# A graph network on one core: 64-column products, kept sums in the messages' place, later layers written out on TensorE

## The reference, cut to what matters

```python
h = relu(layernorm(x))                      # x: 12500 x 64
for l in range(3):
    mlp = lambda z: relu(z @ W1[l] + b1[l]) @ W2[l] + b2[l]
    agg = segment_sum(mlp(h[dst]), src)     # 400000 edges
    h = mlp(h + agg)
out = x + h @ Wf + bf
```

## Time and profile before

| | us |
|---|---|
| median of 3 runs (2140.95 to 2144.04) | 2142.98 |
| the profiled execution | 2147.51 |
| its span | 2145.8 |
| around the span | 1.7 |

### The profile page before, as it was taken

One profiled execution on the slowest core, in us unless ns is written; L12 is line 12 of the kernel. 1 busy time (PEld: TensorE's weight loads), 2 busy tenths in 40 slices (PEclk: granted clock), 3 DMA queues, 4 the chain that ended last, 5 costly groups with the idle time before them and its releaser, 6 DMA issues.

```text
span 2145.8 us, 42350 instructions
## 1 busy us (share of the span) xinstructions
PE 1985.3 (93%) x16959; PEld 1076.8 (50%) x16959; DVE 1442.2 (67%) x1655; ACT 842.3 (39%) x2198; POOL 591.3 (28%) x270
## 2 busy tenths in 40 slices
PE   4566889999999999989999999999999999999998
PEld 3454445555555555544455455455445555555554
DVE  7999999999999999946643443343465444444343
ACT  5986888888888888812200000000010000000000
POOL 2666666666666766600000000000000000000000
PEclk9886999999999999999999999999999999999999
DMA  7356666666666666653544553543544555555452
GB/s 204 95 138 177 187 188 193 191 192 196 191 193 191 196 190 187 197 167 91 157 146 120 165 150 106 178 143 112 165 149 128 167 167 157 160 150 167 137 165 71
DMA packets 332835, 344.60 MB, mean 161 GB/s; under 512 B 21562, under 2 KB 303992, under 8 KB 332184
## 3 DMA queue, kind: packets, MB, share of 16 engines
q1 hardware_dynamic: 327516, 335.59, 54.0%
q0 software_dynamic: 2352, 6.43, 1.1%
q10 hardware_dynamic: 2816, 0.53, 0.2%
HBM read 252.58 MB, written 89.89 MB: 160 GB/s over the span
## 4 chain that ended last, share of the span: by engine, by line
PE 60%; DVE 23%; DMA 7%; issue 5%; POOL 2%; SPq 2%; ACT 1%; ACTq 1%; DVEq 0%; POOLq 0%
PE ps L1552 49%; DVE arena L756 13%; DMA arena<-counts_dram 7%; PE ps L1417 6%; DVE arena L764 5%; POOL arena L633 2%; DVE arena L796 2%; DVE arena L804 2%; PE ps L1502 2%; SPq L457 2%; PE ps L1529 1%; PE ps L1384 1%; ACTq L1105 1%; ACT row_edges L1115 1%; DMA counts_dram<-arena 1%
## 5 line engine op out<-in xcount | busy, mean ns | idle before, releaser
L1552 PE MATMUL ps<-arena,parts 128*128 128x448 fp8e4 x5488 | 1049.4, 353 | 1.4 <-DVE arena L892 1.4
L1552 PEld LDWEIGHTS ps<-arena,parts 128*128 128x128 f16 x5488 | 531.6, 98 | 518.4 <-issue 27.1
L879 DVE TENSOR_SCALAR arena<-arena 128x3136 uint16<-128x3136 uint16 x196 | 191.4, 976 | 586.7 <-PE ps L1552 586.7
L633 POOL TENSOR_TENSOR arena<-arena,weight_now 128x416 int32<-128x416 int32 x196 | 506.8, 2586 | 280.3 <-DVE arena L756 276.4
L1417 PE MATMUL ps<-arena,parts 128*128 128x448 fp8e4 x2744 | 554.2, 354 | 1.8 <-DVE parts L845 1.8
L756 DVE TENSOR_TENSOR arena<-row_iota,key_now 128x3712 f16<-128x3712 f16 (+1 forms) x196 | 415.1, 2118 | 0.0
L1283 ACT ACTIVATE arena<-arena 128x448 f32<-128x448 f32 x42 | 24.2, 577 | 980.6 <-DVE arena L906 980.6
L1417 PEld LDWEIGHTS ps<-arena,parts 128*128 128x128 f16 x2744 | 255.6, 98 | 279.7 <-issue 55.2
L1190 ACT ACTIVATE arena<-ps 128x800 uint16<-128x800 f32 x392 | 340.3, 880 | 23.9 <-PE ps L1384 23.8
L1384 PE MATMUL ps<-arena 128*128 128x53 fp8e4 x6272 | 204.1, 190 | 103.8 <-POOL arena L633 100.7
L1384 PEld LDWEIGHTS ps<-arena 128*128 128x128 f16 x6272 | 191.0, 98 | 167.9 <-DVE arena L756 82.8
(11 more groups left out here) (152 smaller groups left out, 1045.1 us busy)
## 6 DMA issues: line engine op xcount, KB each, us to landing
arena<-counts_dram SPq DMA_DIRECT2D x294, 784.0 KB, 4.8
counts_dram<-arena SPq DMA_DIRECT2D x784, 100.0 KB, 2.3
h_dram<-parts SPq DMA_DIRECT2D x2, 1536.0 KB, 7.2
edges_dram<-arena SPq DMA_DIRECT2D x2, 1400.0 KB
arena<-in_x_dram SPq DMA_DIRECT2D x14, 192.0 KB
out_dram<-arena SPq DMA_DIRECT2D x14, 192.0 KB
arena<-in_dst_dram SPq DMA_DIRECT2D x1, 1400.0 KB
arena<-in_src_dram SPq DMA_DIRECT2D x1, 1400.0 KB
```

The lines of the kernel that those rows point to most:

```text
L633: nc.gpsimd.tensor_tensor(pairs, pairs, weight_now[:, h * HW:(h + 1) * HW].unsqueeze(2).to_broadcast([P, HW, WORDS // 2]), ALU.mult).then_ ...
L879: v.tensor_scalar(spread[:, c % WIDE, 0, :].bitcast(U16), packed, 0x0F0F, None, ALU.bitwise_and)
L1552: last = t.matmul(ps[:, b, 0:NB], parts[:, c * CK + k, :], spread[:, c % WIDE, b // 2, at:at + NB].bitcast(F8), start=start, stop=stop)
```

## The change

- A tile's product has 64 weight columns instead of 128: for each tile, column half (bank) and nibble the upper and the lower parts are multiplied one after the other into the same 64 partitions, the two nibbles into the two halves of the partitions (`multiply_tile`). A stretch uses two banks instead of four (`SBB`), with 8 matmuls of 64 columns a tile instead of 4 of 128.
- `read_sums` and `keep_sums` have two banks; all kept sums now lie in `msg`, and `acc_high` is gone. `add_kept` runs once a unit.
- Within the counting PE does in quarter h one chunk (h // 2) and one bank (h % 2) of the unit. DVE unpacks the first chunk's high nibbles in quarter 0 (before: 1), ahead of the second's low ones, and the second's high nibbles in quarter 1 (before: 2). The waits follow: PE waits for a chunk's high nibbles, DVE's low unpacking of the second chunk for the whole unit before, that of the first for the first chunk's products.
- The u stages of a stretch become one, with four matmuls of 64 x 64; in layer 0's last round the stages stand behind banks 1, 2, 3, 4.
- `ring0` has four buffers. ACT makes four of a quarter's rows (`FEW`).
- PE's loops over the stretches of layers 1 and 2 are written out.

```diff
-FEW = 3
+FEW = 4
...
-SBB = 4
-SBC = NB * SBB
+
+
+SBB = 2
+SBC = NB * SBB * 2
 SBH = SBC // 2
...
-RING0 = 3
+RING0 = 4
...
-BANKS = (0, 2, 1, 3)
...
-        acc_high, at = view(build_end, [SB, 2, NB], F32)
-        ring0, at = view(at, [RING0, CK * SBH], U8)
+        ring0, at = view(build_end, [RING0, CK * SBH], U8)
...
-        zP, at = view(0, [SBC], F32)
+        zP, at = view(0, [SBB * NB], F32)
...
-        acc_low = msg[:].rearrange("p k d -> p (k d)").rearrange("p (s b n) -> p s b n", s=SB, b=2)
+        so_far = msg[:].rearrange("p k d -> p (k d)").rearrange("p (s b n) -> p s b n", s=SB, b=SBB)
         def kept_sums(st, b):
-            return acc_low[:, st, b, :] if b < 2 else acc_high[:, st, b - 2, :]
+            return so_far[:, st, b, :]
...
+        def half(n):
+            return slice(n * D, (n + 1) * D)
+
+        def exchanged(u, b):
+
+            return b * min(u // SB, ROUNDS - 2) % 2
+
+        def swapped(l, b):
+
+            return b * l % 2
...
             def unpack_low(n):
-                u = n // ROUND
                 dve.wait_ge(round_loaded[n % RING0], 16 * (n // RING0 + 1))
-                if u:
-                    dve.wait_ge(s["sums_done"], SBB * (u - 1) + 2)
+                u, c = n // ROUND, n % ROUND
+                if u and c == 0:
+                    dve.wait_ge(s["chunks_multiplied"], u)
+                elif u:
+                    dve.wait_ge(s["sums_done"], SBB * u)
                 v.tensor_scalar(spread[:, n % WIDE, 0, :].bitcast(U16), ring0[:, n % RING0, :].bitcast(U16), 0x0F0F, None,
-                                ALU.bitwise_and).then_inc(s["low_unpacked"], 1)
+                                ALU.bitwise_and)
             def unpack_high(n):
-                u = n // ROUND
-                if u:
-                    dve.wait_ge(s["sums_done"], SBB * u)
                 v.tensor_scalar(spread[:, n % WIDE, 1, :].bitcast(U16), ring0[:, n % RING0, :].bitcast(U16), 4, 0x0F0F,
                                 ALU.logical_shift_right, ALU.bitwise_and).then_inc(s["counts_unpacked"], 1)
...
+                for b in range(SBB):
+                    dve.wait_ge(s["sums_done"], (UNITS - SB + g) * SBB + b + 1)
...
                 if h == 0 and u >= 0:
+                    unpack_high(ROUND * u)
                     unpack_low(ROUND * u + 1)
                 if h == 1 and u >= 0:
-                    unpack_high(ROUND * u)
-                if h == 2 and u >= 0:
                     unpack_high(ROUND * u + 1)
                 if h == 3 and 0 <= unit_of(j + 1) < FUSED:
...
-            def keep_sums(u, b, bank):
+            def keep_sums(u, b):
                 act.wait_ge(s["sums_done"], SBB * u + b + 1)
-                if u < SB and b < 2:
+                if u < SB:
                     act.wait_ge(s["parts_made"], ROUND * (u + 1))
-                a.activation(kept_sums(u % SB, b), ps[:, bank, 0:NB], ACT.Copy,
+                a.activation(kept_sums(u % SB, b), ps[:, b, 0:NB], ACT.Copy,
                              scale=scal[:, 0, 6:7] if u >= UNITS - 2 * SB else 1.0).then_inc(s["sums_kept"], 1)
...
+                b = (k - 1) % HG - (HG - SBB)
+                if k and unit_of((k - 1) // HG) >= 0 and b >= 0:
+                    keep_sums(unit_of((k - 1) // HG), b)
...
-            def add_kept(u, b, bank):
-
-
-                for c in range(2):
+            def add_kept(u):
+
+
+                for b in range(SBB):
                     for r in range(2):
-                        rows, to = slice(r * D, (r + 1) * D), slice((r ^ c) * D, (r ^ c) * D + D)
-                        t.matmul(ps[to, bank + c, 0:NB], ident[rows, rows], kept_sums(u % SB, b + c)[rows], start=True, stop=False)
-
-            def multiply_chunk(u, c, b, bank, stop):
+                        t.matmul(ps[half(r ^ b), b, 0:NB], ident[half(r), half(r)], kept_sums(u % SB, b)[half(r)], start=True,
+                                 stop=False)
+
+            def multiply_tile(tile, wide, k, b, exchange, start, stop):
+
+
+                at = k * SBH + b * NB
+                for part in range(2):
+                    for c in range(2):
+                        last = t.matmul(ps[half(c), b, 0:NB], parts[:, tile, half(part)],
+                                        spread[:, wide, c ^ exchange, at:at + NB].bitcast(F8), start=start and part == 0,
+                                        stop=stop and part == 1)
+                return last
+
+            def multiply_chunk(u, c, b):
                 for k in range(CK):
-                    at = k * SBH + b % 2 * NB
-                    last = t.matmul(ps[:, bank, 0:NB], parts[:, (ROUND * (u // SB) + c) * CK + k, :],
-                                    spread[:, c, b // 2, at:at + NB].bitcast(F8), start=(u < SB or u >= UNITS - SB) and c == 0 and k == 0,
-                                    stop=stop and k == CK - 1)
+                    last = multiply_tile((ROUND * (u // SB) + c) * CK + k, c, k, b, exchanged(u, b),
+                                         (u < SB or u >= UNITS - SB) and c == 0 and k == 0, c == ROUND - 1 and k == CK - 1)
                 return last
-            def add_bank(u, b):
-
-                if b == 0:
+            def add_bank(u, h):
+
+                c, b = h // SBB, h % SBB
+                if h == 0:
                     pe.wait_ge(s["parts_made"], ROUND * (u // SB + 1))
-                if u >= SB and b % 2 == 0:
-                    pe.wait_ge(s["sums_kept"], SBB * u + b)
-                    add_kept(u, b, 0)
-                elif SBB * u + b >= 2:
-                    pe.wait_ge(s["sums_kept"], SBB * u + b - 1)
-                else:
-                    pe.wait_ge(s["hidden0_kept"], BLOCKS)
-                for c in range(ROUND):
-                    pe.wait_ge(s["low_unpacked" if b < 2 else "counts_unpacked"], ROUND * u + c + 1)
-                    last = multiply_chunk(u, c, b, b % 2, c == ROUND - 1)
-                last.then_inc(s["sums_done"], 1)
+                    if u:
+                        pe.wait_ge(s["sums_kept"], SBB * u)
+                    else:
+                        pe.wait_ge(s["hidden0_kept"], BLOCKS)
+                    if u >= SB:
+                        add_kept(u)
+                pe.wait_ge(s["counts_unpacked"], ROUND * u + c + 1)
+                last = multiply_chunk(u, c, b)
+                if c == ROUND - 1:
+                    last.then_inc(s["sums_done"], 1)
+                elif b == SBB - 1:
+                    last.then_inc(s["chunks_multiplied"], 1)
...
-                steps = ["u0", "u1", "own", "", "m0", "m1"] if not final else ["u0", "u1", "", "", "m0", "m1"]
+                steps = ["u", "", "own", "", "m0", "m1"] if not final else ["u", "", "", "", "m0", "m1"]
                 if n >= len(steps) or not steps[n]:
                     return
                 kind = steps[n][0]
                 if kind == "u":
-
-                    b = int(steps[n][1])
-                    wait_alone(pe, s["sums_read"], g * SBB + 2 * b + 2)
-                    for w in range(2):
-                        cols = slice((2 * w + b) * NB, (2 * w + b + 1) * NB)
-                        last = t.matmul(ps[half(w ^ swapped(l, b)), 4 + b, 0:NB], W1s[:, l, :], zP[:, cols], start=True, stop=True)
-                    last.then_inc(s["u_done"], 1)
+                    wait_alone(pe, s["sums_read"], (g + 1) * SBB)
+                    for b in range(SBB):
+                        for r in range(2):
+                            last = t.matmul(ps[half(r ^ b), 4 + b, 0:NB], W1s[half(r), l, :], zP[half(r), b * NB:(b + 1) * NB],
+                                            start=True, stop=True)
+                        last.then_inc(s["u_done"], 1)
...
-                        steps.sort(key=lambda step: BANKS.index(step[1]))
+                        steps.sort(key=lambda step: step[1])
                     for k, b in steps:
                         start, stop = c == 0 and k == 0, c == CH - 1 and k == CK - 1
                         if start:
-                            wait_alone(pe, s["sums_read"], g * SBB + BANKS.index(b) + 1 - SBB)
-                        at = k * SBH + b % 2 * NB
-                        last = t.matmul(ps[:, b, 0:NB], parts[:, c * CK + k, :],
-                                        spread[:, c % WIDE, b // 2, at:at + NB].bitcast(F8), start=start, stop=stop)
+                            wait_alone(pe, s["sums_read"], g * SBB + b + 1 - SBB)
+                        last = multiply_tile(c * CK + k, c % WIDE, k, b, b ^ swapped(l, b), start, stop)
                         if stop:
                             last.then_inc(s["sums_done"], 1)
...
-            MLP_AT = {2: (0, 1), 4: (2,), 6: (4,), 7: (5,)}
+            MLP_AT = {1: (0,), 2: (2,), 3: (4,), 4: (5,)}
             pe.wait_ge(s["weights_fused"], 2)
             for u in range(FUSED, UNITS):
                 i = u - (UNITS - SB)
-                banks = range(SBB) if i < 0 else BANKS
```

(46 more changed lines are left out.)

2 lines of the change are left out of this document (1 added, 1 removed).

## The result

The changed kernel takes 2125.57 us (median of 4 runs, 2120.89 to 2127.72), the kernel before 2143.51 (4 runs, 2140.95 to 2144.40): ratio 0.9911, 95% interval 0.9894 to 0.9928. The forecast was 2127. The profiled execution took 2123.59, its span is 2121.9.

What follows compares the result with a forecast made beforehand. DVE was taken to bound the counting up to about 912 us, PE layers 1 and 2. Terms 3.0 - 14.0 - 3.7 + 0.5 - 0.9 - 10.7 + 10 = -15.8 from 2143.0 gave 2127 us, range 2108 to 2170.

Steps and rivals of the forecast that it cites:

- Pairs at a product's price: In all layers, two 64-column matmuls run side by side at a product's 0.1895 us; +3.0 us in the sum.
- Rival A: Each pair of matmuls costs 7 ns more than a product: +39 us, 2166 us, slower; chance 0.14.
- C: The fp8 halves do not overlap, 3636 us, or the weight loads lose their cover, about 2900 us; chance 0.07.
- The loads' own time: On PE, a weight load of 64 columns takes an estimated 53 ns, two in a row 107, and stays hidden.
- The u stage: On PE, one stage per stretch instead of two saves 1.00 us in each of 14 stretches: -14.0 us.
- The rest of layer 0: Shorter u stages in layer 0's last round save 3.7 us; adding kept sums once instead of twice saves 0.9 us.
- The end: In the last stretch u waits for all sums, where half of it ran ahead before: +0.5 us.
- The fourth row: In the counting, ScalarE takes one more row and DVE's comparison shrinks by 65 ns in 164 groups: -10.7 us.
- The moved unpackings: In the counting, DVE wants the first chunk's load 1.0 us sooner; its idle for loads grows to about 21: +10 us.
- Writing out the loops: PE's loops over stretches of layers 1 and 2: no idle at a loop's turn, so writing them out brings nothing.
- PE within the counting: PE needs 16.0 us of each unit's 17.3 after the change, so DVE stays the bound: 0.
- Rival B: PE's instruction supply bounds the counting at 43 ns each, 21.5 us a unit: +172 us, 2299 us; chance 0.11.

Runs made afterwards that it cites:

- e4: The changed kernel with its u stage cut into two stages of two 64 x 64 matmuls each: 2137.4 us, ratio 0.9958.
- e1: The changed kernel with three rows on ScalarE again (FEW = 3): 2132.85 us, ratio 0.9940.
- e8: The kernel before with four rows on ScalarE (FEW = 4) and five window buffers instead of six: 2136.52 us, ratio 0.9955.
- e2: The changed kernel with three buffers for the rounds' loads (RING0 = 3) instead of four: 2125.02 us, ratio 0.9912.
- e11: The kernel before with PE's loops over the stretches of layers 1 and 2 written out: 2144.91 us, ratio 0.9997.
- e3: The changed kernel with PE's loops over stretches 1 to 6 of layers 1 and 2 put back: 2216.07 us, ratio 1.0319.
- e7: The changed kernel with each late stretch's sixth chunk multiplied for one nibble half first, then for the other: 2193.45 us, ratio 1.0224.
- e10: The kernel before with two stretches in each turn of PE's loops of layers 1 and 2: 2165.64 us, ratio 1.0095.

## Why the prediction was right, step by step

- **Two stages with two bounds**: held. All of the late gain came from PE's path, and the counting followed DVE's.
- **Pairs at a product's price**: held. 14 stages at 1.0 and the 13.3 measured leave 0.7 us for 5488 pairs, 0.13 ns each, and e4 against the kernel before leaves 0.9 us, 0.16 ns each; +2.7 was forecast for them. Rival A is out, at 7 ns a pair and at the 4 that the prediction names beside it: the second matmul starts 3 ns behind the first, and that does not add to the pitch. So is C. The weight loads, doubled in number, stay hidden, as costed.
- **The loads' own time**: from the Trainium skill ("TensorE: Matmul & The Clock Gate", LDWEIGHTS) an estimate of 53 ns was given. The loads of 64 columns take 110 ns, longer than the 98 of 128 columns. The page's formula is too low by half here. Nothing hung on it: two loads in a row would be 220 ns and stick out of a pitch of 0.19 us, but their records overlap (56 loads in 5.3 us would need 6.2 in a row), and the pitch is unchanged.
- **The u stage**: -14.0 forecast, e4 measured 14.2.
- **The rest of layer 0**: -3.7 and -0.9 forecast, 4.4 measured against the runs' mean of 109.4. The sixth stage's gain was lost as forecast; the wait at layer 1's start grew from 1.36 to 1.94:

```profile
1027.43 2.84 PE L1428 MATMUL ps<-arena,parts 128*64 128x448 fp8e4 x28 [1.94 <-DVE arena L901]
```

- **The end**: +0.5 forecast, 0.5 in the profiled pair, up to 1.4 in the other runs with one u stage. e4, with two, is back at the 12.7 of before, so the place was right.
- **The fourth row**: 65 ns less forecast. The comparison went from 2086 to 2016, 70 ns, 11.5 us of DVE's time in 164 quarters, of which 7 to 8 arrive. The rest comes back as waiting: from e1 to the changed kernel 1.6 us more for loads, 1.1 for PE and 1.4 for stores; in e8 not for loads but for ScalarE (7.3 us, above).

```profile
L766 DVE TENSOR_TENSOR arena<-row_iota,key_now 128x3584 f16<-128x3584 f16 x164 | 330.6, 2016 | 0.0
```

- **The moved unpackings**: the term that was mis-sized. +10 forecast, with waits for loads of about 21 us; 6 measured, with waits of 16.1. Mechanism and place were right (the waits in front of the low unpacking grew, and go when the loads go sooner), the shift of all 82 unpackings was not: when DVE stops for one load, the next is issued no later but wanted later, and the sum over single loads counts that twice. This last reason is argued, not shown.
- **The fourth buffer**: nothing, as forecast (e2).
- **Writing out the loops**: "nothing" was right for the kernel before (e11), but for a reason that the prediction did not see. It took the absence of idle at the turns for a property of loops; it is one of short loops. The prediction never asked what the changed kernel would be without that edit, and called it free where it is worth 90 us. The same reasoning would have given the same forecast for e3, 90 us too low; that the edit was part of the change is why this did not show.
- **PE within the counting**: 16.0 us of 17.3 a unit forecast, no wait of DVE for it beyond 1.9 us. Rival B is out: PE is idle 34 of the 460 us, at 35 ns a record over the whole stretch, and DVE is still the bound.
- **The sum**: -15.8 forecast, -17.9 between the medians and -23.9 between the two profiled executions, of which some 3 lie in the kernel before's long counting (736.7 against a mean of 733.8) and 1.5 in the start. In the counting the two terms, -10.7 and +10, were both too large, by about 3 and 4 us, and cancelled: -0.7 forecast, -1.3 measured. That part of the hit is luck.

## What to carry to other kernels

An fp8 product with 64 weight columns costs half of one with 128 if its neighbour in PE's queue writes to the other half of the partitions, and all of it if the other half's matmuls stand far off (e7); so a sum of two parts can be formed in PSUM for the same PE time, and what that saves is found in the stages that it shortens, not in the products. When an edit doubles the instructions of a loop on PE, look whether the loop still stays where the instructions are kept: instruction packets inside a loop and "issue" idle at its turns say no. Count a transfer's lead from what its queue issues ahead of it before buying it a buffer.

## What the runs showed of the hardware

- A PE loop of some 800 instructions a turn (392 matmuls and their loads, the kernel before) draws no instruction packets after its first turn, in layer 1 and in layer 2; one of some 1600 draws them all through and stands 3.1 to 5.1 us at its turns (e3, e10), with half clock behind it at all ten turns of e3 and at two of the four of e10. Where between the two the limit lies was not tried.
- Instruction packets in straight code do not stop PE: 94 in layers 1 and 2 of the changed kernel, without an idle.
- Weight loads of 64 fp16 columns take 110 ns, those of 128 take 98.
- Two 64-column matmuls for different halves of the partitions overlap as neighbours, and one also starts ahead of three of the other half that stand before it in the queue, and of no more, in all 14 chunks (e7). A pair's pitch is 0.19 us, that of one 128-column matmul.
- A stage of f32 matmuls of 64 x 64 over 448 columns lasts 0.97 us with two and 0.98 us with four (e4, changed).
